# Causal attention: the mask moves from a TensorE matmul into VectorE's row maximum

## The reference

```python
k = jnp.einsum('ihd,bpd->biph', W_K, x)
q = jnp.einsum('ihd,bpd->biph', W_Q, x)
v = jnp.einsum('ihd,bpd->biph', W_V, x)
scores = jnp.einsum('biph,biqh->biqp', k, q)
mask = jnp.tril(jnp.ones((pos, pos), dtype=x.dtype))
masked = scores * mask - jnp.float32(10000000000.0) * (1.0 - mask)
attn = jax.nn.softmax(masked / jnp.sqrt(jnp.float32(d_head)), axis=-1)
z = jnp.einsum('biqp,biph->biqh', attn, v)
```

## Time and profile before

| | |
|---|---|
| time, median of 3 runs | 1408.63 us (1407.89 to 1410.15) |
| profiled execution | span 1405.0 us, first to last instruction; no other time is given for it |
| PE busy | 1328.9 us, 95% |
| DVE busy | 905.6 us, 64% |
| ACT busy | 722.3 us, 51% |
| POOL busy | 571.1 us, 41% |

### The profile page before, as it was taken

How to read it: one execution, slowest core, us unless ns; L and a number is a source line. 1 busy time by engine, 2 the same in 40 slices (tenths; PEclk the granted TensorE clock), 3 DMA queues, 4 the chain that set the end, 5 groups by cost and what they waited for, 6 DMA issues and landing times.

```text
span 1405.0 us, 28535 instructions
## 1 busy us (share of the span) xinstructions
PE 1328.9 (95%) x8578; PEld 1171.3 (83%) x8578; DVE 905.6 (64%) x1875; ACT 722.3 (51%) x1688; POOL 571.1 (41%) x587
## 2 busy tenths in 40 slices
PE   5999999999999899999999999999889997989998
PEld 4888888888888787888778888888779887978886
DVE  5667666666667878687886666666776632345536
ACT  2655555555555555554445555555455553545443
POOL 5535535355232223213043635441003664546554
PEclk9999999999999999999999999999999998999999
DMA  3253544525533000000001201020459996899963
GB/s 118 83 173 105 188 164 133 172 97 183 164 135 102 19 20 16 16 16 20 12 31 60 66 27 68 34 86 0 151 202 311 368 337 237 307 363 378 302 200 116
DMA packets 128246, 195.98 MB, mean 139 GB/s; under 512 B 10400, under 2 KB 99744, under 8 KB 128160
## 3 DMA queue, kind: packets, MB, share of 16 engines
q1 hardware_dynamic: 64752, 110.04, 23.4%
q10 hardware_dynamic: 51120, 51.26, 10.9%
q0 software_dynamic: 12288, 33.57, 6.8%
HBM read 107.79 MB, written 87.03 MB: 139 GB/s over the span
## 4 chain that ended last, share of the span: by engine, by line
PE 82%; DVE 7%; issue 3%; ACT 3%; DMA 3%; another core or an unknown queue 1%; SPq 1%; ACTq 0%; POOL 0%; POOLq 0%; DVEq 0%
PE ps_s L782 9%; PE ps_t L841 8%; PE ps_s L784 8%; PE ps_s L783 8%; PE ps_x L782 6%; PE ps_x L783 6%; PE ps_x L784 6%; PE ps_z L782 5%; PE ps_z L784 5%; PE ps_z L783 5%; PE ps_t L1006 3%; PE ps_z L1006 3%; PE ps_s L975 2%; PE ps_t L782 2%; PE ps_t L783 2%
## 5 line engine op out<-in xcount | busy, mean ns | idle before, releaser
L1116 ACT ACTIVATE prob<-ps_s,neg_max 128x128 f32<-128x128 f32 (+7 forms) x256 | 189.4, 741 | 256.3 <-DVE neg_max L1312 252.1
L1327 DVE TENSOR_TENSOR pT_lo<-ps_t,pT_hi 128x512 fp32r<-128x512 f32 (+2 forms) x320 | 189.4, 603 | 104.9 <-ACT pT_hi L1132 101.3
L1132 ACT ACTIVATE pT_hi<-ps_t 128x512 fp32r<-128x512 f32 (+2 forms) x320 | 161.4, 533 | 94.8 <-PE ps_t L841 92.1
L1312 DVE TENSOR_REDUCE neg_max<-ps_s 128x1 f32<-128x128 f32 (+7 forms) x256 | 186.8, 748 | 14.0 <-PE ps_s L784 11.5
L679 POOL DMA_INDIRECT xs<-xn,slots x128 | 127.7, 997 | 134.8 <-PE ps_z L1006 67.6
L841 PE MATMUL ps_t<-ident,prob 128*128 128x128 f32 x1152 | 170.8, 274 | 9.4 <-ACT prob L1116 4.2
L841 PEld LDWEIGHTS ps_t<-ident,prob 128*128 128x128 f32 x1152 | 136.7, 140 | 33.1 <-DVE pT_lo L1327 5.7
L782 PE MATMUL ps_s<-k_hi,q_hi 128*128 128x512 f32 (+2 forms) x384 | 154.7, 403 | 0.0
L1524 DVE TENSOR_TENSOR h<-sg,ps_s 128x256 f32<-128x256 f32 x112 | 46.9, 418 | 155.9 <-ACT sg L1166 103.9
L782 PE MATMUL ps_s<-ring,a_hi 128*128 x384 | 125.5, 327 | 14.3 <-SPq L530 11.9
L784 PE MATMUL ps_s<-k_hi,q_lo 128*128 128x512 f32 (+2 forms) x384 | 133.7, 348 | 0.0
(11 more groups left out here) (306 smaller groups left out, 3682.9 us busy)
## 6 DMA issues: line engine op xcount, KB each, us to landing
ring<-ws SPq DMA_DIRECT2D x56, 512.0 KB
xs<-taken SPq DMA_DIRECT2D x16, 1536.0 KB, 9.8
xq<-xs ACTq DMA_DIRECT2D x48, 512.0 KB
xs<-yq ACTq DMA_DIRECT2D x48, 512.0 KB
ws<-split_to SPq DMA_DIRECT2D x34, 512.0 KB, 3.1
raw<-experts_dram SPq DMA_DIRECT2D x34, 256.0 KB, 3.4
raw_a<-w_a_dram SPq DMA_DIRECT2D x15, 512.0 KB, 4.4
ring_down<-experts_dram SPq DMA_DIRECT2D x56, 128.0 KB
```

The source lines that it names most:

```text
L1116: act.activation(prob[c][:, j, 0:width(r)], ps_s[r % 2][:, 0:width(r)], ACT.Exp, bias=neg_max[:, r:r + 1], accum_out=row_sum[:, c, j:j + 1 ...
L1132: act.activation(to, ps_t[m % 2][:, j * P:], ACT.Copy).then_inc(s_hi, 1)
L1312: dve.tensor_reduce(neg_max[:, r:r + 1], ps_s[r % 2][:, 0:width(r)], AX.X, ALU.max, negate=True).then_inc(s_max, 1)
L1327: dve.tensor_tensor(lo, ps_t[m % 2][:, j * P:], hi.bitcast(F32), ALU.subtract).then_inc(s_bank_free, 1)
```

## The change

The mask matmul goes. VectorE's instruction adds the mask, multiplies by -1, writes the row back to where it was in PSUM and takes the row's minimum, which is the negated maximum; the exponential then reads the negated row with a scale of -1. The mask buffer is 1024 columns wide, zeros with the triangle in the last 128, so that its last `width(r)` columns fit any row. A semaphore increment of VectorE's own stands ahead of the instruction (no one waits for it). To make room in SBUF, buffers of the routing part share memory: `earlier` becomes a corner of `below`, `rank` and `kept` become `pair_a` and `pair_b`, the router's weights are loaded into `score`, `number_int` into `owner`.

```diff
-    ident, ident_bf = sb("ident", [P, P]), sb("ident_bf", [P, P], BF16)
-    causal = sb("causal", [P, P], BF16)
+    ident, causal = sb("ident", [P, P]), sb("causal", [P, S], BF16)
...
+    rw = score[:, 0:ND, :]
...
-    rank, kept = sb("rank", [P, NT, G]), sb("kept", [P, NT, G])
+    rank, kept = pair_a, pair_b
...
+    earlier = below[:, 0:G, 0:G]
...
-        for m in (ident, ident_bf):
+        for m in (ident,):
...
-        pool.affine_select(out=causal[:, :], in_=causal[:, :], compare_op=ALU.is_ge, fill=MASKED,
+        own = causal[:, S - P:]
+        pool.affine_select(out=own, in_=own, compare_op=ALU.is_ge, fill=MASKED,
                            base=0, pattern=[[-1, P]], channel_multiplier=1).then_inc(s_const, 1)
...
             to = ps_s[r % 2]
-            pe.matmul(to[:, r * P:(r + 1) * P], ident_bf[:, :], causal[:, :], start=True, stop=False,
-                      skip_group_check=True)
             for k0 in range(0, width(r), NQ):
                 k1 = max(min(width(r), k0 + NQ), k0 + 2 * P)
-                diagonal = k0 <= r * P < k1
                 last = three(to[:, k0:k1], q_hi[a][:, q], q_lo[a][:, q], k_hi[a][:, k0:k1],
-                             k_lo[a][:, k0:k1], not diagonal, True, diagonal)
+                             k_lo[a][:, k0:k1], True, True)
...
             act.activation(prob[c][:, j, 0:width(r)], ps_s[r % 2][:, 0:width(r)], ACT.Exp,
-                           bias=neg_max[:, r:r + 1],
+                           bias=neg_max[:, r:r + 1], scale=-1.0,
                            accum_out=row_sum[:, c, j:j + 1]).then_inc(s_exp, 1)
...
             dve.wait_ge(s_scores, row + 1)
-            dve.tensor_reduce(neg_max[:, r:r + 1], ps_s[r % 2][:, 0:width(r)], AX.X, ALU.max,
-                              negate=True).then_inc(s_max, 1)
+            dve.sem_inc(s_masking, 1)
+            row_of = ps_s[r % 2][:, 0:width(r)]
+            dve.tensor_tensor_reduce(out=row_of, in0=row_of, in1=causal[:, S - width(r):], scale=-1.0, scalar=LARGEST,
+                                     op0=ALU.add, op1=ALU.min, accum_out=neg_max[:, r:r + 1]).then_inc(s_max, 1)
...
+        dve.wait_ge(s_const, 6)
         for kind, k, n, m in walk(START):
```

More of the change, by code:

```diff
@@ L20 @@
 MASKED = -1.0e30
+LARGEST = 3.0e38
 NEVER = -3.0e38
@@ L316, in build @@
     row_sum, inv_sum = sb("row_sum", [P, NC, BC]), sb("inv_sum", [P, NC, BC])
-    rw, bias_bc = sb("router_w", [P, ND, E]), sb("bias_bc", [P, E])
+    bias_bc = sb("bias_bc", [P, E])
     rw_hi, rw_lo = sb("router_hi", [P, ND, E], F32R), sb("router_lo", [P, ND, E], F32R)
-    earlier = sb("earlier", [P, G, G])
     score, biased = sb("score", [P, NT, E]), sb("biased", [P, NT, E])
+    rw = score[:, 0:ND, :]
     pair_a, pair_b, group = sb("pair_a", [P, NT, G]), sb("pair_b", [P, NT, G]), sb("group", [P, NT, G])
-    rank, kept = sb("rank", [P, NT, G]), sb("kept", [P, NT, G])
+    rank, kept = pair_a, pair_b
     best, taken = sb("best", [P, NT, 8]), sb("taken", [P, NT, E])
@@ L332, in build @@
     tiles, base, end = sb("tiles", [P, E]), sb("base", [P, E]), sb("end", [P, E])
-    number_int = sb("number_int", [1, TILES], mybir.dt.int32)[:, :]
     number, owner = sb("number", [1, TILES]), sb("owner", [1, TILES])
+    number_int = owner[:, :].bitcast(mybir.dt.int32)
     need = [sb(f"need{b}", [1, TOPK], mybir.dt.int32) for b in range(B)]
@@ L424, in build @@
     s_scores, s_max, s_exp = sem("scores"), sem("max"), sem("exp")
+    s_masking = sem("rows_being_masked")
     s_bank, s_hi, s_bank_free = sem("bank"), sem("pT_hi"), sem("bank_free")
@@ L450, in build @@
     WS0, YS0 = 16, 16
-    CONSTS = 25 + WORD
+    CONSTS = 21 + WORD
     X_SCORES = [X0 + x_before + count_of(order, ("M", b, 0)) + 1
@@ L478, in _ @@
                 .then_inc(s_load[n], 16)
-        sp.dma_start(rw[:, :, :], router).then_inc(s_in, 16)
+        sp.dma_start(rw, router).then_inc(s_in, 16)
         sp.dma_start(bias_bc[:, :], bias.partition_broadcast(P)).then_inc(s_in, 16)
@@ L578, in _ @@
         pool.memset(zero[:, :], 0.0).then_inc(s_const, 1)
-        pool.memset(ident_bf[:, :], 0.0).then_inc(s_const, 1)
         pool.memset(causal[:, :], 0.0).then_inc(s_const, 1)
-        pool.wait_ge(s_const, 5)
-        for m in (ident, ident_bf):
+        pool.wait_ge(s_const, 4)
+        for m in (ident,):
             pool.affine_select(out=m[:, :], in_=m[:, :], compare_op=ALU.not_equal, fill=1.0,
                                base=0, pattern=[[-1, P]], channel_multiplier=1).then_inc(s_const, 1)
-        pool.affine_select(out=causal[:, :], in_=causal[:, :], compare_op=ALU.is_ge, fill=MASKED,
+        own = causal[:, S - P:]
+        pool.affine_select(out=own, in_=own, compare_op=ALU.is_ge, fill=MASKED,
                            base=0, pattern=[[-1, P]], channel_multiplier=1).then_inc(s_const, 1)
@@ L631, in _ @@
         pool.wait_ge(s_in, 32)
-        split(flat(rw_hi), flat(rw_lo), flat(rw), 4, s_router)
+        split(flat(rw_hi), flat(rw_lo), rw.rearrange("p a b -> p (a b)"), 4, s_router)
         pool.memset(pL_hi[:, 0:P].bitcast(F32), 0.0).then_inc(s_const, 1)
@@ L639, in _ @@
         pool.memset(below[:, :, :], 1.0).then_inc(s_const, 1)
-        pool.memset(earlier[:, :, :], 1.0).then_inc(s_const, 1)
         pool.memset(gain[:, :], 0.0).then_inc(s_const, 1)
@@ L646, in _ @@
         pool.iota(thr_int, pattern=[[P, NT]], base=0, channel_multiplier=0).then_inc(s_const, 1)
-        pool.wait_ge(s_const, 18 + 1 + WORD)
+        pool.wait_ge(s_const, 15 + 1 + WORD)
         pool.tensor_copy(number[:, :], number_int).then_inc(s_const, 1)
@@ L654, in _ @@
                            base=0, pattern=[[1, E], [-1, E]], channel_multiplier=0).then_inc(s_const, 1)
-        pool.affine_select(out=earlier[:, :, :], in_=earlier[:, :, :], compare_op=ALU.is_gt, fill=0.0,
-                           base=0, pattern=[[1, G], [-1, G]], channel_multiplier=0).then_inc(s_const, 1)
         def split_v1(p, count, x_before):
@@ L777, in _, with three @@
         pe.sem_inc(s_pv, PV0)
[L778 to L784, removed]
+        pe.wait_ge(s_const, 6)
+        def three(to, w_hi, w_lo, m_hi, m_lo, start, stop):
+            pe.matmul(to, w_hi, m_hi, start=start, stop=False)
+            pe.matmul(to, w_hi, m_lo, start=False, stop=False)
+            return pe.matmul(to, w_lo, m_hi, start=False, stop=stop)
         def transpose_xn(q, d, bank):
@@ L1395, in route @@
                 step(dve.tensor_tensor(level, level,
-                                       earlier[:, :, :].unsqueeze(1).to_broadcast([P, NT, G, G]),
+                                       earlier.unsqueeze(1).to_broadcast([P, NT, G, G]),
                                        ALU.mult))
```

## The result

The changed kernel took 1393.38 us (median of 4 runs, 1392.24 to 1394.15), the kernel before, run beside it, 1408.26 us: a ratio of 0.9898, 95% interval 0.9871 to 0.9924. The time lies inside the wide range that was given (1376 to 1406) and 2 us above the forecast's own range (1377 to 1391): 14.9 us were gained where 26.2 were forecast.

The account below looks back on a forecast made before the run. TensorE was taken as the bound, with 82% of the chain. Masks gain 29.9 us, less 1.9, 1.2 and 0.6: 26.2 us, so 1408.6 - 26.2 = 1382 us; range 1376 to 1406, own range 1377 to 1391.

Parts of the forecast that it names:

- 29.9 - 1.9: Attention: 256 mask matmuls off TensorE gain 29.9 us, less 1.9 us for 16 masks worth nothing in 420 to 720 us.
- 1.2 + 0.6: Longer maximum: 1.2 us lost at 8 maxima on the chain in 420 to 720 us, 0.6 us in 720 to 960 us.
- the deductions for 420 to 720 us: Pairs that also normalise, route and dispatch: 1.9 us for masks worth nothing, 1.2 us for 8 longer maxima.
- The step that failed: Steady pair, R0.2, R0.3, then transpose T1.0: two rows late by 0.15 us each use 0.30 of 0.42, so nothing is lost.
- The slack of 0.42 us: Steady pair: time between the end of ScalarE's last read, 282.31, and the start of transpose T1.0, 282.73.
- The mask's price: TensorE in attention: each mask matmul costs 0.10 us behind a transpose, 0.13 behind a matmul; 1.87 us a pair.
- The maximum's price: VectorE's new instruction: 0.15 us more a row, 0.10 for the accumulator's read and 0.05 for the increment; bounds 0 and 0.25.
- 4 late places: In 720 to 960 us TensorE already waits for ScalarE's exponential at 4 places; each loses 0.15 us, 0.6 us together.
- C: Rival: VectorE needs a second pass to write the PSUM row, 1.05 ns more per column; slower, 1420 us; chance 0.16.
- B: Rival: VectorE's fixed cost is larger, 0.4 us a row, so T1.0 stalls; 1391 us, 1396 with 0.5; chance 0.12.
- D: Rival: no change, something hidden refills the mask's slot on TensorE; within 3 us of 1408.6; chance 0.06.
- A: The forecast itself: 1382 us, own range 1377 to 1391; chance 0.66.

## Why the prediction was right in sign and too large in size

**The ledger**, in us of attention. Masks: forecast 29.9 - 1.9 = 28.0; measured 1009.91 - 988.12 = 21.8. New instruction: forecast 1.2 + 0.6 = 1.8; measured 995.73 - 988.12 = 7.6 with the masks gone, 1016.69 - 1009.91 = 6.8 with them there. Together 26.2 forecast, 14.2 measured. Of the 7.6 and 6.8, 3.0 and 2.9 lie in pairs 11 to 14, which move by as much between two executions of one kernel; outside them it is 4.6 and 3.9.

By place, the 12.0 us that are missing are 4.0 in pairs 0 to 5 (6 x 0.67), 0.4 in pair 6, 2.6 in pairs 7 to 10 (with the deductions for 420 to 720 us put there), 3.4 in pairs 11 to 14 and 1.6 in the first and last pieces. The chain to T1.0 explains 0.49 of each 0.67, so 2.9 of the first 4.0.

**The step that failed** is the sentence "No mask lies between R0.3 and T1.0, so the shorter PE stream takes none of that slack." R0.3's scores are not what VectorE waits for; R0.1's are the last. Behind them lie the masks of R0.2 and R0.3, and so PE's way to T1.0 became shorter than the chain's: PE gained 0.46 us from T0.0 to T1.0, the start of R0.1's maximum only 0.21 with its scores. The slack of 0.42 us was spent twice: 0.25 on the masks and 0.33 on the new instruction (the chain from T0.0 ends at 10.35 us, and at 10.02 without any mask and with the old reduce). That is 0.16 too much, and with the 0.06 between ScalarE's read and the transpose T1.0 waits 0.23 us; the places behind it lose another 0.26.

**The mask's price** of 0.10 to 0.13 us was right: between T0.0 and V0.2 four masks gave 0.46 us, 0.115 each. What was wrong was to credit each slot in full.

**The maximum's price** of 0.15 us a row was too high for most rows, and counted in the wrong place. I had put 0.10 on the accumulator's read and 0.05 on the increment. The read's row is 143 ns, but the exponential starts 91 ns after the main instruction's end and started 34 ns after the reduce's (where ScalarE is free; both worked out from starts and durations): 0.06 us. The main instruction is 0.01 to 0.05 longer. The increment is nothing when VectorE is behind; when VectorE waits, the new instruction starts 0.16 us later behind the scores than the reduce did (0.20 against 0.04 us), and a second increment adds 0.09, so the first one's own share of the 0.16 is not separated. That makes 0.07 to 0.11 us in most rows and 0.24 in the few that wait. The prediction took its 50 ns for the increment from no row, on the ground that VectorE waits in the wide rows; it waited for scores in 38 of the 256. For T1.0 its 2 x 0.15 = 0.30 came close to the 0.33 by luck: set against the run without any mask, the new instruction delays the exponential of R0.1 by 0.19 us and that of R0.3 by a further 0.13, and R0.0 and R0.2 add nothing. What failed was to count the price only in 420 to 720 us and at 4 late places: in the steady pairs it costs 0.25 to 0.34 us, because the slack was gone.

The Trainium skill (VectorE: DVE Perf Modes, Two Vector instructions with no wait between them) has the accumulator's read as an instruction of its own. The trace agrees: 256 rows of it, 143 ns each. The 62 cycles more for PSUM sources in the same page (The TRN2 errata) do not show in the earlier trace rows: 1024 columns took 1215 ns within SBUF and 1221 out of PSUM. For a row that is written back into PSUM the new instruction's fixed part is 291 - 128 x 1.07 = 154 ns, where the reduce, which also reads PSUM, has 146.

**Pairs 8 to 10** were to gain 3 x 1.87 less some deductions. With no mask at all and the old reduce they gain 1.9 us together, so two thirds of the masks there were off the path, and the new instruction takes 1.8 of that back.

**The rivals.** C (a second pass, slower) is excluded by the slope of 1.07 ns a column. B has the symptom that it named, an unchanged slope and PE waiting at T1.0, but not its cause: the fixed cost is about 0.1 us or less in most rows. (The argument against B that all VectorE rows lie on one line does not hold for all: `acc<-ps_t,inv_sum,acc` takes 474 ns on 256 columns in the kernel before, where the line gives 415.) D is excluded: a pair is 1.20 us shorter. The time fell 2 us above A's own range, where B's 1391 to 1396 stood, by A's mechanism with a wrong slack; that it still lies in the wide range is owed to the range's width, since little more than half of the forecast gain came.

**Still open**: what VectorE waits for in pairs 11 to 14. Between two executions of the same kernel it made 2.9 us (239.70 - 236.85), a quarter of the 12 us that are missing. In pairs 6 to 10 and in the last pair the chains were not followed item by item; that the same happens there is not shown.

## What to carry to other kernels

To say that an engine has slack at a wait, follow the waited-for chain back to the last point where it hangs on that engine, and subtract everything that the change takes out of the engine's stream since that point: the slack of a chain is shortened by every microsecond saved beside it. Here the last such point was R0.1's scores, and 0.25 us of masks lay behind it. Then look at the next two or three places fed by the same queue, since a wait that is just avoided at one reappears behind it. And test it by shortening an unrelated link of the suspected chain, in both kernels: if only one gets faster, the path has moved.

## What the hardware showed unexpectedly

An in-place, two-operand VectorE instruction on PSUM with a reduction beside it runs at the reduce's rate (1.07 against 1.05 ns a column), and its accumulator's read of 143 ns costs the consumer 0.06 us. With an increment of a semaphore between the wait and the instruction, VectorE starts 0.20 us after the scores when it has to wait for them (0.04 with the reduce and no increment), a second increment adds 0.09, and neither costs anything that can be seen when VectorE is behind. PE's busy share of 359.63 in 360 us held a wait of 0.23 us in each pair that neither the busy columns nor the list of PE's waits shows; the weight loads' waits show that it is there, and the distance between starts what it costs.
